# Graph attention, then a gated expert layer: the spread of the neighbour scores set behind the probability transposes of its slot

## The reference, cut to what matters

```
h  = layernorm(x); Wh = h @ W.T                    # [16, 1024, 256]
e  = leaky_relu((Wh @ a1)[:, :, None] + (Wh @ a2)[:, None, :], 0.2)
e  = where(adj == 0, -inf, e)
x  = x + softmax(e, axis=-1) @ Wh                  # attention over the neighbours
f  = layernorm(x)                                  # then eight experts of three layers each,
w  = softmax(mean(f, axis=0) @ Wr + br)            # gated per node
x  = x + sum_e w[:, e] * (relu(bn(relu(bn(f @ W1[e])) @ W2[e])) @ Wo[e] + bo[e])
```

## Time and profile before

| what | value |
|---|---|
| time, median of 3 runs | 2852.62 us (2850.52 to 2852.64) |
| the profiled execution's own time | 2852.83 us |
| its span | 2851.0 us |
| busy over the span: PE, DVE, ACT, POOL | 97%, 85%, 75%, 24% |
| busy from 100 to 628 us (528 us of the attention part): PE, DVE, ACT, POOL | 499.06, 483.98, 471.30, 441.45 us |
| the same from 700 to 2850 us (2150 us of the expert part) | 2130.86, 1785.03, 1526.63, 125.73 us |
| granted TensorE clock from 100 to 628 us | 1.00 of full speed |

### The profile page before, as it was taken

The page is one execution under the profiler, slowest core; times in us unless marked ns, Lnnn a source line. Parts: engine busy times, 40 slices in busy tenths (PEclk is TensorE's granted clock), DMA queues, the critical chain, the costliest instruction groups (busy, mean ns, idle before and its releaser), DMA issues.

```text
span 2851.0 us, 48981 instructions
## 1 busy us (share of the span) xinstructions
PE 2778.1 (97%) x17110; PEld 2467.3 (87%) x17110; DVE 2414.6 (85%) x3567; ACT 2134.7 (75%) x3038; POOL 691.9 (24%) x953
## 2 busy tenths in 40 slices
PE   7999999999899999999999999999999999999998
PEld 6889889889788888888888888888888888888887
DVE  7999999998788888888888888888888888888887
ACT  6889889888677777777777777777777777777775
POOL 5888888888100000000000000000000000001000
PEclk9999999999999999999999999999999999999999
DMA  4444444443345454454455455555455445545444
GB/s 145 155 159 147 156 157 147 155 158 114 125 163 165 152 168 163 152 170 163 155 160 164 155 159 164 153 167 164 154 166 165 156 158 163 161 154 162 158 157 138
DMA packets 160012, 445.27 MB, mean 156 GB/s; under 512 B 16032, under 2 KB 73800, under 8 KB 159840
## 3 DMA queue, kind: packets, MB, share of 16 engines
q1 hardware_dynamic: 159840, 442.98, 48.5%
HBM read 401.99 MB, written 40.93 MB: 155 GB/s over the span
## 4 chain that ended last, share of the span: by engine, by line
PE 72%; DVE 1%; ACT 1%; issue 0%; POOL 0%; DVEq 0%; ACTq 0%; POOLq 0%
PE head_ps L52 12%; PE head_ps L54 12%; PE head_ps L53 12%; PE m_ps L1208 7%; PE m_ps L1211 7%; PE m_ps L1210 7%; PE z_ps L54 4%; PE z_ps L52 4%; PE z_ps L53 4%; PE turn_ps L1183 1%; PE turn_ps L1191 1%; ACT h L1338 0%; DVE h_sums L1491 0%; DVE h_lo L1484 0%; DVE h_lo L1450 0%
## 5 line engine op out<-in xcount | busy, mean ns | idle before, releaser
L1338 ACT ACTIVATE h<-head_ps,bn_shift,bn_scale 128x512 f32<-128x512 f32 x768 | 594.0, 774 | 534.4 <-PE head_ps L54 326.2
L1484 DVE TENSOR_TENSOR h_lo<-h_sums,h_hi 128x1792 fp32r<-128x1792 f32 x256 | 518.2, 2024 | 200.4 <-ACT h_hi L1352 200.3
L1352 ACT ACTIVATE h_hi<-h_sums 128x1792 fp32r<-128x1792 f32 x256 | 435.2, 1700 | 65.3 <-DVE h_sums L1504 61.7
L86 POOL TENSOR_TENSOR ffn_vareps<-ffn_mv,ln_eps 128x4 f32<-128x4 f32 x32 | 7.9, 246 | 1862.3 <-DVE ffn_mv L80 1862.3
L1491 DVE TENSOR_TENSOR h_sums<-h,gate_row 128x1024 f32<-128x1024 f32 x256 | 313.7, 1225 | 121.1 <-ACT h L1338 103.0
L1450 DVE TENSOR_TENSOR h_lo<-h,h_hi 128x1024 fp32r<-128x1024 f32 x256 | 311.8, 1218 | 6.9 <-ACT h_hi L1365 6.9
L52 PE MATMUL attn_ps<-wh_hi,pT_hi 128*128 128x256 f32 x1024 | 303.9, 297 | 0.0
L53 PE MATMUL attn_ps<-wh_lo,pT_hi 128*128 128x256 f32 x1024 | 286.9, 280 | 0.0
L54 PE MATMUL attn_ps<-wh_hi,pT_lo 128*128 128x256 f32 x1024 | 286.8, 280 | 0.0
L1365 ACT ACTIVATE h_hi<-h 128x1024 fp32r<-128x1024 f32 x256 | 270.9, 1058 | 0.1
L1208 PE MATMUL m_ps<-h_hi,wo_ops 128*128 128x256 f32 x896 | 257.0, 287 | 4.0 <-DVE h_lo L1484 4.0
(11 more groups left out here) (198 smaller groups left out, 7887.2 us busy)
## 6 DMA issues: line engine op xcount, KB each, us to landing
wh_lo<-wo_scratch SPq DMA_DIRECT2D x124, 896.0 KB, 6.3
wo_ops<-wo_scratch SPq DMA_DIRECT2D x124, 896.0 KB, 6.5
adj_sb<-in_adj SPq DMA_DIRECT2D x128, 512.0 KB, 3.5
gate_row<-w_scratch SPq DMA_DIRECT2D x256, 256.0 KB, 4.6
x_sb<-in_x SPq DMA_DIRECT2D x64, 256.0 KB, 2.8
x_scratch<-x_sb SPq DMA_DIRECT2D x128, 128.0 KB, 1.8
ffn_x<-x_scratch SPq DMA_DIRECT2D x16, 512.0 KB, 7.6
x_sb<-x_scratch SPq DMA_DIRECT2D x16, 512.0 KB, 7.6
```

The source lines that it names most:

```text
L1338: return act.activation(dst, src, ACT.Relu, bias=bn_shift[layer][:, col], scale=bn_scale[layer][:, col])
L1352: act.activation(h2_hi[s % 2][:, :, :], g2[:, 1:8, :], ACT.Copy).then_inc(S["h2_hi_ready"], 1)
L1484: dve.tensor_tensor(h2_lo[s % 2][:, :, :], g2[:, 1:8, :], bits(h2_hi[s % 2][:, :, :]), ALU.subtract) \
```

## The change

Nothing is added or removed; three pieces of the slots with step 5 (slots 2 and 10 of a pair, 15 times in all) move:

- TensorE: `spread_ej` goes from before the probability transposes to behind them, ahead of the attention matmuls.
- ScalarE: `head_ej` goes from before the relu to behind `upper_half` (the copy to `pT_hi`).
- VectorE: the mask of that slot goes from before `pT_lo` to behind it. In all other slots it stays.

```diff
@@ TensorE, slot(k, u, last_pair)
                 head = head_at(k, u, last_pair)
-                if head and head[1] == HEADS + 1:
-                    spread_ej(2 * k + head[0], head[0] % 2)
                 ok, t, n = tile_at(k, u, 3, last_pair)
                 if ok:
                     pe.wait_ge(S["probs_ready"], n)
...
                     last.then_inc(S["pT_ready"], 1)
+                if head and head[1] == HEADS + 1:
+                    spread_ej(2 * k + head[0], head[0] % 2)
@@ ScalarE, slot(k, u, last)
-                if head and head[1] == HEADS + 1:
-                    head_ej(2 * k + head[0], head[0] % 2)
                 if head and 1 <= head[1] <= HEADS:
...
                 else:
                     relu(k, u, last)
                     upper_half(k, u, last)
+                    if head and head[1] == HEADS + 1:
+                        head_ej(2 * k + head[0], head[0] % 2)
@@ VectorE, slot(k, u, last): the mask's lines become mask()
+                def mask():
+                    ok, t, n = tile_at(k, u, 6, last)
+                    if ok:
...
+                if step != HEADS + 1:
+                    mask()
                 ok, t, n = tile_at(k, u, 3, last)
                 if ok:
...
                     dve.tensor_tensor(pT_lo[t % 2][:, :, :], pT_ps[t % 2][:, :, :], bits(pT_hi[t % 2][:, :, :]),
                                       ALU.subtract).then_inc(S["pT_lo_ready"], 1)
+                if step == HEADS + 1:
+                    mask()
```

More of the change, by code:

```diff
@@ L905, in slot @@
                     head_stats(2 * k + stats[0], stats[1], stats[0] % 2, k + (stats[0] // 2 + 1))
[L906 to L914, removed]
+                def mask():
+                    ok, t, n = tile_at(k, u, 6, last)
+                    if ok:
+                        dve.wait_ge(adj_in[t % 2], DMA * (k * (UT // 2) + (t // 2 + 1)))
+                        if t % TB == 0:
+                            dve.wait_ge(S["ej_rows_ready"], 2 * k + (t // TB + 1))
+                        wait(dve, S["pT_ready"], n - 4)
+                        dve.scalar_tensor_tensor(scores[t % 4][:, :], adj_sb[t % 2][:, :], 0.0, ej_rows[parity(t)][:, :],
+                                                 ALU.is_equal, ALU.add).then_inc(S["masked_ready"], 1)
+                if step != HEADS + 1:
+                    mask()
                 ok, t, n = tile_at(k, u, 3, last)
```

## The result

The changed kernel takes 2876.93 us (median of 4 runs, 2874.13 to 2878.32), the kernel before 2852.63 us in the same comparison: ratio 1.0086, 95% interval 1.007 to 1.0101. It is slower, as forecast, but by 24.3 us and not by 9.1, and outside the range (to 2865). Its profiled execution is the shortest of the four: 2874.13 us, with a span of 2872.3 us, 21.3 over the span before.

The account below looks back on a forecast made before the run. The prediction took VectorE's arrival at `wh_lo` to set each batch, with GpSimd bounding that slot by a little. 14 batches x 0.65 us = 9.1 us on 2852.62 gave 2861.7 us; range 2848 to 2865, forecast's own range 2857.5 to 2865.

Parts of the forecast that it names:

- What bounds the kernel: VectorE's arrival at `wh_lo`, four slots after the spread, sets a batch's length; TensorE waits there 14 times, 15.3 us.
- ScalarE and VectorE: In the spread slot: exponential 319.89, `pT_lo` 318.33, mask 319.47, leaky step 320.67; the 0.96 us stall brings 0.06.
- TensorE's later attention matmuls: Behind the spread: start 317.88 instead of 317.39, 0.49 us later, hidden by TensorE's 0.94 us idle before 321.23.
- GpSimd: Spread to fourth slot: masks and leaky steps hold its chain; reciprocal at 335.45, before 334.62, so VectorE 0.83 us later.
- The variance: GpSimd's variance at 324.66, 0.09 behind the leaky step of 324.57, was to be held by it to 325.64.
- the mask, later by itself: VectorE's mask due at 326.77, 0.18 behind GpSimd's sum of 326.59, was to be held to 327.21.
- The price of that lateness: At `wh_lo`: 0.83 - 0.18 = 0.65 us later per batch, in 14 batches 9.1 us.
- a pure shift: After the fourth slot's reciprocal: `xs_vareps` and everything later only shift, because TensorE waits for `wh_lo` anyway.
- No rival: GpSimd keeps pace 2848.1, GpSimd unreordered 2849.2 (together 0.20); VectorE alone 2845.6 (0.10); whole stall 2837.5 (0.02); earlier tie 2857.9 (0.12).
- Port rule: Spread slot: by the letter the variance would hold the leaky step 0.07 us per batch, 1 us in all: 2862.7.
- taking 0: Spread slot: the hold of the leaky step of 320.67 by GpSimd's variance was taken as 0, both bounds giving nothing.
- SP: Load of the adjacency tile two slots later starts 2.07 us later, lands by about 324.5, needed at 326.77: hidden.

Follow-up runs that it names:

- experiments 8 to 10: `wh_lo` computed ahead of `pT_lo` in two slots: in the kernel before 2835.05 us, in the changed kernel with late weight subtraction 2831.72, in the changed kernel 2845.16.
- experiment 1: Changed kernel plus 14 unused TensorE transposes ahead of the x transposes that wait for `wh_lo`: 2865.12 us against 2852.01, ratio 1.0047.
- experiment 4: Kernel before plus three unused statistics instructions on VectorE ahead of `wh_lo`, 1.0 us later there: 2875.77 us, ratio 1.0082.
- experiment 5: Kernel before plus three unused VectorE statistics instructions ahead of `wh_lo` and 14 unused TensorE transposes in front of the wait: 2865.91 us, ratio 1.0046.
- experiment 3: Kernel before with GpSimd's weight subtraction at the end of slots 7 and 15 instead of 4 and 12: 2852.94 us, ratio 1.0002.
- experiment 2: Changed kernel with GpSimd's weight subtraction at the end of slots 7 and 15 instead of 4 and 12: 2847.65 us, ratio 0.9982.
- experiment 6: Changed kernel with the mask back in its old place ahead of `pT_lo`, spread and copies still moved: 2867.89 us, ratio 1.0057.
- experiment 7: Kernel before with only the mask of the spread slot moved behind `pT_lo`: 2874.3 us (two runs only), ratio 1.0076.

## Why the prediction was wrong

- **What bounds the kernel: right.** Shown by experiments 8 to 10: two slots with another order on VectorE brought 17.2 us in the kernel before.
- **ScalarE and VectorE: right.** Exponential, `pT_lo`, mask and first leaky step came within 0.08 us of their worked places (counted from the spread). TensorE's later attention matmuls were hidden.
- **GpSimd: right in the mechanism and the sum, wrong in one place on the way.** The holds on the inverse root, the sum of the spread slot and `xs_vareps` came as worked out. The reciprocal one slot on also waited 0.23 us for `row_den` (333.29), which I had not followed; this moved VectorE back by 0.27. The variance then passed ahead of the leaky step (333.15 and 333.37), where the forecast had it held, but the inverse root was held behind it, and the sum began where it was worked out. So the mask, later by itself, was held by 0.15 and not 0.44. The two errors cancel at the fourth slot, 18.42 us against 18.44, and that the agreement is so close is luck.
- **The price of that lateness: right, with that luck in it.** 0.65 a batch and 9.1 us forecast, 0.69 and 9.6 us measured in the batches at full clock, and 9.5 in experiment 1.
- **"What `xs_vareps` and everything after the reciprocal cost is a pure shift: TensorE waits for `wh_lo` anyway": this step failed.** It priced a longer wait by its length only. Behind the longer wait TensorE ran at half its clock in nine of 14 batches, 1.53 us each, 13.8 us: more than the lateness itself. The sum has no term for this. Experiments 1, 4 and 5 show that the longer wait is the cause. No rival had it, so the range missed as well. The forecast even named the wait's growth (from 15.3 to about 25 us; it was 28.5, since TensorE also gets there 0.24 us earlier) without asking what a wait of 2 us does. The Trainium skill (TensorE: Matmul & The Clock Gate, section "Part 1: The HAM clock gate") says that a monitor of TensorE's recent activity sets its clock to full or half; the traces agree, with 1.00 and 0.50 as the only two values.
- **Port rule.** The skill's lock for the whole instruction (SBUF — State Buffer, "SBUF: two separate sides") would have held the leaky step of 329.14 until the variance's end. It started 0.06 before that instruction's recorded end and took its plain 1.21 us, so taking 0 was right. But this row does not test the rule: GpSimd's sum, too, let a leaky step go 0.11 before its recorded end. What speaks against the letter of the rule is still the inverse root at 320.39.
- **SP: hidden.** The one wait of a mask for an adjacency tile (0.40 us at 27.34, ahead of the batches) is in the kernel before too (0.41 at 28.77).

What stays open: why the clock fell behind nine of these waits and not behind the other five of the same length (1.98 us ahead of 261.43, clock kept; 1.97 ahead of 349.79, clock halved). All falls of the clock in these batches, nine after and six in experiment 4, begin between 0.13 us before and 0.78 us behind the end of their wait. Since waits of one length end both ways, where a wait lies in time may decide; that is not shown. The experiments vary the idle time, not where it lies.

## What to carry to other kernels

A stall that is taken away pays only if the engine is earlier at the place that sets the period; here 15 us of stall were worth nothing by themselves and 5.3 us with GpSimd relieved (experiment 3 against 2), and a reordering next to it moved a queue that no semaphore of the change touches. Follow each engine that the moved instructions hold, slot by slot, with the lead of one start over the other, not by busy time. And where TensorE's wait grows, ask for its clock too: a kernel can pay more for the clock behind a wait than for the wait, and the first test is to fill the wait with idle work.

## What the runs showed of the hardware

- Waits of TensorE of 0.96 to 1.38 us once in a batch never lowered its clock in the 14 batches (the kernel before, experiments 3, 6 and 7); waits of 1.96 to 2.14 us did in nine of 14 batches after the change and in six of 14 in experiment 4.
- VectorE's leaky step and mask (two inputs in SBUF) and GpSimd's instructions hold each other by order of start: GpSimd's sum held a leaky step that began 0.10 us behind it by 0.51 us, and a mask held the `xs_vareps` that began 0.10 us behind it (1.17 us for 0.19). GpSimd's 0.55 us inverse root does not hold a leaky step that starts 0.18 us behind it, but is held itself if it starts 0.14 behind.
- Removing load from GpSimd can cost VectorE: experiment 3 gave back in a hold of the leaky step (0.28 us) more than it won in the wait (0.18 us).
